# Second attention: a share of the squares one operation later on VectorE, and the weighted sums copied out by VectorE

## The chip, the cores and the metric

The program runs on one NeuronCore of one Trainium2 chip. The metric is the device time of one execution in microseconds (us); of three timed executions of the kernel before the median is 3164.51 us (3160.64 to 3164.62). Engines: PE is TensorE, DVE is VectorE, ACT is ScalarE, POOL is GpSimd, SP is SyncE, which only issues DMAs here.

## The reference

The model has six sublayers on 4 x 1024 tokens of width 128: a top-1 expert layer, causal attention, the top-1 expert layer again, a top-2 expert layer, a second attention with two kinds of weights, and the top-2 expert layer again. The change lies in the second attention alone (16 heads of width 8, no mask):

```python
S = jnp.einsum('bhnd,bhmd->bhnm', Q, K) / dh ** 0.5
W_tau = jax.nn.softmax(S, axis=-1)
W_sigma = 1.0 / ((1.0 + jnp.abs(S) / b_) ** 2 + t_ ** 2)
W_sigma = W_sigma / W_sigma.sum(axis=-1, keepdims=True)
tau   = jnp.einsum('bhnm,bhmd->bhnd', W_tau, V)
sigma = jnp.einsum('bhnm,bhmd->bhnd', W_sigma, V)
f = 0.5 * tau + 0.5 * sigma
```

## The kernel before, in words

`attend_both` runs the second attention. The batch and the heads give 64 heads to go through; each has 1024 queries and 1024 keys, in 8 tiles of 128. A *slot* is two tiles, so a head is four slots and the stage 256. Every engine runs its own loop over slots, written out by hand; semaphores alone tie them together, and each engine takes its instructions strictly in the order written. Within one body `j` different jobs belong to different slots (lags `LS` = 4, `LT` = `LE` = 6, `LP` = 7).

Per slot, each of the two halves `i`:

- PE computes three times a 128 x 1024 tile of scores: into `pm` for the row maxima, into `pb` for the softmax (with the negated maximum carried in extra rows of the stack), into `pa` for the absolute values. Then it *weighs*: `weigh` multiplies `Vh` (128 x 32) with the weights of an earlier slot and adds into `po` (L1786, 8 matmuls).
- DVE takes the row maximum of `pm` (L1927) and clears the sign of `pa` into the buffer `sg` (L1936). There are one `pm`, one `pa` and one `pb`, so PE waits with each until it has been read.
- ACT takes the exponential of `pb` into `pt` (L1849), and on the whole slot the logarithm and the exponential that make 1/(square + constant) out of the square (L1864, L1868).

The square is z(z + b), elementwise over a slot's 2 x 1024 columns. Its first 26/32 are POOL's, in two instructions: `shifted = z + b` (L1727) and `z * shifted` (L1730). The last 6/32 are DVE's, one `scalar_tensor_tensor` of 128 x 384 elements (L1942). Both engines read and write SBUF only here, and both wait for the second sign clearing of the slot.

Once a head, in these four slots (A is the slot with `j % 4 == 0`, then B, C, D):

- Slot D: PE finishes the head's last weighing in the first half (`pv_done`); the sums `po` (128 x 512) are copied to `osb` by ACT (L1856); the first weighing of the next head, in the second half of D, may not write `po` before (`pe.wait_ge(o_sb, h)`); after it PE transposes `osb` (L1832) into `ptr`.
- Slot A: `output` on DVE, four small instructions that divide by the sums and write the head's result (L1903 to L1914). In its second half PE transposes the maxima (L1817), and at the end of the slot DVE runs `negated`, four small instructions on 8 x 128 (L1883 to L1890) whose rows SP's DMAs put into the stacks.

DVE's row of a slot is thus: maximum, [`output`], sign, maximum, sign, square, [`negated`].

Of the kernel before, what the change touches and what calls it, by code (L numbers as in the profile page):

```python
# [11 lines left out]
ALU = mybir.AluOpType  # L12
ACT = mybir.ActivationFunctionType
# [3 lines left out]
B, T, D = 4, 1024, 128  # L17
# [3 lines left out]
TT = T // P  # L21
# [11 lines left out]
RING = 4  # L33
# [1605 lines left out]
def attend_both(nc, tag, V, F, par, qd, kd, ident, stacks, cleared):  # L1639
# [6 lines left out]
    PER = TT // 2  # L1646
    UNROLL = PER * RING
    LS, LT, LE, LP = 4, 6, 6, 7
    SC = DH ** -0.5
    CUT = 26 * T // 32  # L1650
    with ExitStack() as ctx:
# [3 lines left out]
        parh = m.sb("parh", [P, RING, 2])  # L1655
# [3 lines left out]
        sg = [m.sb(f"sg{r}", [P, 2, T]) for r in range(4)]  # L1659
        shifted = m.sb("shifted", [P, 2, CUT])  # L1660
        osb = m.sb("osb", [P, CH])
# [5 lines left out]
        po = m.ps("po", [P, CH])  # L1667
# [12 lines left out]
        def at(it, j, lag):  # L1680
            s = UNROLL * it + (j - lag)
            return None if isinstance(s, int) and not 0 <= s < SLOTS else s

        def head(it, j, lag):

            return RING * it + (j - lag) // PER
# [10 lines left out]
        def some(x, least=1):  # L1697

            return not (isinstance(x, int) and x < least)

        with nc.Block() as block:
# [136 lines left out]
            @block.scalar  # L1838
            def _(act):
                nc.scalar.preload_act_table_set("natural_log_exp_and_others")  # L1840

                def body(it, j):
                    st, se, so = at(it, j, LT), at(it, j, LE), at(it, j, LP + 1)
                    for i in range(2):
                        if st is not None:
                            act.wait_ge(tau_mm, 2 * st + i + 1)
                            if some(st, 4):
                                act.wait_ge(pv_done, 2 * (st - 4) + i + 1)
                            nc.scalar.activation(pt[(j - LT) % 4][:, i, :], pb[:], ACT.Exp, scale=SC)\  # L1849
                                .then_inc(tau_exp, 1)  # L1850
                        if i == 0 and so is not None and (j - LP - 1) % PER == PER - 1:
                            h = head(it, j, LP + 1)
                            act.wait_ge(pv_done, TT * h + TT)
                            if some(h):
                                act.wait_ge(o_turned, h)
                            nc.scalar.activation(osb[:], po[:], ACT.Copy).then_inc(o_sb, 1)  # L1856
                        if se is not None:
                            buf = sg[(j - LE) % 4]
                            if i == 0:
                                h = head(it, j, LE)  # L1860
                                act.wait_ge(sq_pool, se + 1)
                                act.wait_ge(sq_dve, se + 1)
                                act.wait_ge(par_ready, h + 1)
                                nc.scalar.activation(buf[:], buf[:], ACT.Ln,  # L1864
                                                     bias=parh[:, ((j - LE) // PER) % RING, 1:2]).then_inc(ln_done, 1)
                            else:
                                act.wait_ge(ln_done, se + 1)
                                nc.scalar.activation(buf[:], buf[:], ACT.Exp, scale=-1.0).then_inc(sig_done, 1)  # L1868

                slots(act, body)  # L1870

            @block.vector
            def _(dve):
                def negated(it, j):

                    if j % PER or at(it, j, 1) is None:
                        return
                    h, r = head(it, j, 1), ((j - 1) // PER - 1) % RING
                    top, rem = ptr[0:TT, 0:P], ptr[0:TT, P:2 * P]
                    dve.wait_ge(rows_turned, h + 1)  # L1880
                    if some(h):
                        dve.wait_ge(rows_in[r], 16 * SPLIT * (it + ((j - 1) // PER - 1) // RING + 1))
                    nc.vector.tensor_scalar(rows[:, 0, :], top, -1.0, None, ALU.mult).then_inc(chain, 1)  # L1883
                    dve.wait_ge(chain, 3 * h + 1)
                    nc.vector.scalar_tensor_tensor(rem, top, -1.0, rows[:, 0, :], ALU.mult, ALU.subtract)\
                        .then_inc(chain, 1)
                    dve.wait_ge(chain, 3 * h + 2)
                    nc.vector.tensor_copy(rows[:, 1, :], rem).then_inc(chain, 1)
                    dve.wait_ge(chain, 3 * h + 3)
                    nc.vector.tensor_tensor(rows[:, 2, :], rem, rows[:, 1, :], ALU.subtract).then_inc(rows_sb, 1)  # L1890

                def output(it, j, n):

                    if (j - LP - 2) % PER != PER - 1 or at(it, j, LP + 2) is None:
                        return
                    h = head(it, j, LP + 2)
                    o = ptr[:].rearrange("p (c q k) -> p c q k", c=4, q=4)
                    scale = rz[:].unsqueeze(3).broadcast_to([P, 4, 4, DH])
                    if n == 0:
                        dve.wait_ge(o_turned, h + 1)  # L1900
                        if some(h):
                            dve.wait_ge(weighed, 2 * h)
                        nc.vector.reciprocal(rz[:], o[:, :, :, DH]).then_inc(rz_done, 1)  # L1903
                    if n == 1:
                        dve.wait_ge(rz_done, h + 1)
                        if some(h):
                            dve.wait_ge(f_done, h)
                        nc.vector.tensor_tensor(fw[:], o[:, :, 0:2, 0:DH], scale[:, :, 0:2], ALU.mult)\
                            .then_inc(weighed, 1)
                        nc.vector.tensor_tensor(o[:, :, 2:4, 0:DH], o[:, :, 2:4, 0:DH], scale[:, :, 2:4], ALU.mult)\  # L1910
                            .then_inc(weighed, 1)
                    if n == 2:
                        dve.wait_ge(weighed, 2 * h + 2)
                        nc.vector.tensor_tensor(F[:, :, h, :].rearrange("p (s c) d -> p s c d", s=2),  # L1914
                                                o[:, :, 2:4, 0:DH].rearrange("p c s d -> p s c d"),
                                                fw[:].rearrange("p c s d -> p s c d"), ALU.add)\
                            .then_inc(f_done, 1)

                def body(it, j):
                    sm, ss = at(it, j, 0), at(it, j, LS)  # L1920
                    for i in range(2):
                        if sm is not None:
                            t = 2 * (j % PER) + i
                            dve.wait_ge(max_mm, 2 * sm + i + 1)
                            if i == 0 and j % PER == 0 and some(sm, 2 * PER):
                                dve.wait_ge(rows_turned, head(it, j, 0) - 1)
                            nc.vector.tensor_reduce(mx[:, (j // PER) % 2, t:t + 1], pm[:], AX.X, ALU.max)\  # L1927
                                .then_inc(max_red, 1)
                        if i == 0:
                            for n in range(3):  # L1930
                                output(it, j, n)
                        if ss is not None:
                            dve.wait_ge(abs_mm, 2 * ss + i + 1)
                            if some(ss, 4):
                                dve.wait_ge(pv_done, 2 * (ss - 4) + i + 1)
                            nc.vector.tensor_scalar(sg[(j - LS) % 4][:, i, :].bitcast(I32), pa[:].bitcast(I32),  # L1936
                                                    SIGN_OFF, None, ALU.bitwise_and).then_inc(abs_done, 1)
                    if ss is not None:
                        h, buf = head(it, j, LS), sg[(j - LS) % 4]
                        dve.wait_ge(abs_done, 2 * ss + 2)  # L1940
                        dve.wait_ge(par_ready, h + 1)
                        nc.vector.scalar_tensor_tensor(buf[:, :, CUT:T], buf[:, :, CUT:T],  # L1942
                                                       parh[:, ((j - LS) // PER) % RING, 0:1], buf[:, :, CUT:T],
                                                       ALU.add, ALU.mult).then_inc(sq_dve, 1)
                    negated(it, j)

                slots(dve, body)
        m.clear_sems()

# [167 lines left out]
```

## Time and profile before

| | |
|---|---|
| time, median of 3 | 3164.51 us |
| the profiled execution: its time, its span | 3132.56 us, 3130.8 us |
| busy share of the span | PE 80%, DVE 82%, ACT 72%, POOL 64% |
| second attention, first to last square on DVE | 1273.92 to 2803.41 us |
| DVE squares (L1942) | 256, mean 914 ns, from 617 to 2669 ns |
| POOL (L1727, L1730) | 256 each, mean 1838 and 3733 ns |

How to read it: busy shares are averages over stages with different limits. In the 40 slices of the span, the second attention fills slices 17 to 35, where DVE shows 9 tenths everywhere, and so do ACT and POOL. Below, a timeline row gives the start (us from the span's start), the duration (us), engine, line, operation, output<-input and count; a value in square brackets is how long the engine sat idle before it and what ended that.

### The profile page before, as it was taken

The numbers are of one execution on the slowest core, as the hardware profiler recorded it, in microseconds if no ns is written. First come the engines' busy times: TensorE is split into PE (matmuls) and PEld (weight loads), VectorE is DVE, ScalarE is ACT, GpSimd is POOL, SyncE is SP. The second block draws the span as 40 slices with busy tenths as digits, with TensorE's granted clock in tenths as the row PEclk, the third lists the DMA queues.
The fourth block names the chain that finished last, engine by engine and source line by source line (L and its number), as shares of the span: only waits on it lengthen the run. The fifth ranks groups of instructions, "written<-read, shape, count | busy, mean of one in ns | idle before, by whom it ended". The sixth has DMA issues, their size and how long they took to land. (4 is left out here: it accounts for less than half of the span.)

```text
span 3130.8 us, 61223 instructions
## 1 busy us (share of the span) xinstructions
PE 2497.2 (80%) x18663; PEld 1032.7 (33%) x18790; DVE 2578.9 (82%) x4251; ACT 2257.5 (72%) x2453; POOL 1995.7 (64%) x1350
## 2 busy tenths in 40 slices
PE   3655999997658984788888888888888888874899
PEld 3632333334654552122222222222222222213455
DVE  4666888885566656899999999999999999977665
ACT  4432777776444543599999999999999999992454
POOL 4510222222634441699999999999999999983444
PEclk9976999998778996799999999999999999995899
DMA  3222100010210002000000000000000000000000
GB/s 114 68 74 71 30 28 29 28 29 8 64 51 1 1 0 88 14 15 12 12 13 14 12 12 14 13 12 12 14 13 12 12 15 12 12 1 1 4 11 14
DMA packets 77234, 74.71 MB, mean 24 GB/s; under 512 B 16112, under 2 KB 57592, under 8 KB 76992
## 3 DMA queue, kind: packets, MB, share of 16 engines
q1 hardware_dynamic: 72832, 64.47, 7.0%
q0 software_dynamic: 4288, 8.82, 0.9%
q8 instruction: 59, 0.97, 0.1%
q14 instruction: 55, 0.45, 0.0%
HBM read 48.04 MB, written 24.42 MB: 23 GB/s over the span
## 5 line engine op out<-in xcount | busy, mean ns | idle before, releaser
L1730 POOL TENSOR_TENSOR a_sg<-a_sg,a_shifted 128x1664 f32<-128x1664 f32 x256 | 955.6, 3733 | 21.4
L1927 DVE TENSOR_REDUCE a_mx<-a_pm 128x1 f32<-128x1024 f32 x512 | 619.4, 1210 | 21.9 <-PE a_pm L1769 21.8
L1936 DVE TENSOR_SCALAR a_sg<-a_pa 128x1024 int32<-128x1024 int32 x512 | 619.2, 1209 | 4.2 <-PE a_pa L1769 3.9
L1849 ACT ACTIVATE a_pt<-a_pb 128x1024 f32<-128x1024 f32 x512 | 523.6, 1023 | 108.4 <-PE a_pb L1769 108.4
L1786 PE MATMUL a_po<-a_pt,a_Vh 128*32 128x512 f32 x2048 | 540.6, 607 | 2.2 <-ACT a_sg L1868 2.2
L1786 PE MATMUL a_po<-a_sg,a_Vh 128*32 128x512 f32 x2048 | 540.6, 607 | 0.0
L1727 POOL TENSOR_SCALAR a_shifted<-a_sg,a_parh 128x1664 f32<-128x1664 f32 x256 | 470.4, 1838 | 101.9 <-DVE a_sg L1936 64.2
L1864 ACT ACTIVATE a_sg<-a_sg,a_parh 128x2048 f32<-128x2048 f32 x256 | 511.9, 2000 | 0.0
L1868 ACT ACTIVATE a_sg<-a_sg 128x2048 f32<-128x2048 f32 x256 | 489.9, 1914 | 0.0
L1769 PE MATMUL a_pm<-all_K,all_Q 96*128 96x512 bf16 x1024 | 316.2, 391 | 149.9 <-DVE a_mx L1927 123.8
L1548 ACT ACTIVATE a_pt<-a_ring 128x1024 f32<-128x1024 f32 (+2 forms) x384 | 313.5, 846 | 167.4 <-PE a_ring L1475 164.1
L1625 DVE TENSOR_REDUCE a_mx<-a_ring 128x2 f32<-128x1024 f32 (+3 forms) x384 | 359.2, 955 | 77.2 <-PE a_ring L1458 52.8
L1769 PE MATMUL a_pa<-all_Q,all_K 96*128 96x512 bf16 x1024 | 311.4, 386 | 83.1 <-DVE a_sg L1936 65.9
L1383 POOL TENSOR_SCALAR_AFFINE_SELECT a_pt<-a_pt 128x256 f32<-128x256 f32 x256 | 104.0, 406 | 372.3 <-ACT a_pt L1548 372.0
L1769 PE MATMUL a_pb<-all_Q,all_K 128*128 128x512 bf16 x897 | 279.8, 381 | 13.7 <-ACT a_pt L1849 6.0
L1942 DVE SCALAR_TENSOR_TENSOR a_sg<-a_sg,a_parh 128x384 f32<-128x384 f32 x256 | 233.9, 914 | 15.7 <-POOL a_parh L1716 2.7
L1769 PEld LDWEIGHTS a_pm<-all_K,all_Q 96*128 96x128 bf16 x1024 | 63.6, 98 | 546.0 <-DVE a_mx L1927 522.7
L881 ACT ACTIVATE f_sg<-f_psg 128x512 f32<-128x512 f32 x176 | 105.1, 597 | 167.9 <-PE f_psg L840 166.9
L1492 PE MATMUL a_po<-a_pt,a_Vh 128*32 128x384 f32 (+3 forms) x1920 | 191.4, 437 | 1.9 <-POOL a_pt L1383 1.8
L804 POOL TENSOR_TENSOR f_hidl<-f_hid,f_hidh 128x512 f16<-128x512 f32 x88 | 101.9, 1157 | 124.5 <-ACT f_hidh L888 124.5
L1769 PEld LDWEIGHTS a_pa<-all_Q,all_K 96*128 96x128 bf16 x1024 | 79.5, 97 | 272.9 <-DVE a_sg L1936 232.3
L804 POOL TENSOR_TENSOR all_V<-f_hid,all_XNT 128x512 f16<-128x512 f32 x88 | 101.8, 1157 | 97.1 <-ACT all_XNT L888 97.1
(278 smaller groups left out, 4718.6 us busy)
## 6 DMA issues: line engine op xcount, KB each, us to landing
all_Q<-q_parts SPq DMA_DIRECT2D x256, 48.0 KB
all_K<-k_parts SPq DMA_DIRECT2D x256, 48.0 KB
k_parts<-p_parts SPq DMA_DIRECT2D x16, 384.0 KB, 2.8
all_Q<-a_rows SPq DMA_DIRECT2D x384, 2.0 KB
e_recs<-routed_rows SPq DMA_DIRECT2D x70, 64.5 KB, 1.8
n_xn<-expert_rows SPq DMA_DIRECT2D x16, 256.0 KB, 4.9
q_parts<-p_parts SPq DMA_DIRECT2D x16, 192.0 KB, 2.3
q_parts<-p_parts SPq DMA_DIRECT2D x8, 384.0 KB, 2.6
```

Of the source, the lines that this page charges most:

```text
L1548: nc.scalar.activation(pt[n % 4][:, :, ga:gb, c * P:CH], of_weight(y)[:, :, 0:(gb - ga) * width].rearrange("p u (g n) -> p u g n", n=width ...
L1625: nc.vector.tensor_reduce(mx[:, j % 2, half, :, strip_at(t)], of_maximum(y)[:, :, 0:min(CH, (t + 1) * P - half * CH)], AX.X, ALU.max).then ...
L1727: nc.gpsimd.tensor_scalar(shifted[:], buf[:, :, 0:CUT], b2, 1.0, ALU.add, ALU.mult)\
L1730: nc.gpsimd.tensor_tensor(buf[:, :, 0:CUT], buf[:, :, 0:CUT], shifted[:], ALU.mult)\
L1769: last = nc.tensor.matmul(out[:, lo:lo + CH], lhsT[0:rows_, t * P:(t + 1) * P], rhs[0:rows_, lo:lo + CH], start=True, stop=True)
L1786: last = nc.tensor.matmul(po[32 * q:32 * q + 32, :], Vh[:, ((j - lag) // PER) % 2, t, :], wts[:, i, half * CH:(half + 1) * CH], start=(t = ...
L1849: nc.scalar.activation(pt[(j - LT) % 4][:, i, :], pb[:], ACT.Exp, scale=SC)\
L1864: nc.scalar.activation(buf[:], buf[:], ACT.Ln, bias=parh[:, ((j - LE) // PER) % RING, 1:2]).then_inc(ln_done, 1)
L1868: nc.scalar.activation(buf[:], buf[:], ACT.Exp, scale=-1.0).then_inc(sig_done, 1)
L1927: nc.vector.tensor_reduce(mx[:, (j // PER) % 2, t:t + 1], pm[:], AX.X, ALU.max)\
L1936: nc.vector.tensor_scalar(sg[(j - LS) % 4][:, i, :].bitcast(I32), pa[:].bitcast(I32), SIGN_OFF, None, ALU.bitwise_and).then_inc(abs_done, 1)
L1942: nc.vector.scalar_tensor_tensor(buf[:, :, CUT:T], buf[:, :, CUT:T], parh[:, ((j - LS) // PER) % RING, 0:1], buf[:, :, CUT:T], ALU.add, AL ...
```

## The change

It does two things on DVE's and ACT's rows of the second attention; PE's and POOL's rows stay as they are. DVE's square of a slot no longer stands at the end of its slot but in the next slot's body, behind that slot's first maximum (the function `square`, called in the first half). The copy of `po` to `osb` leaves ACT's slot D and stands on DVE in slot D, behind the second maximum (`copy_out`).

```diff
@@ scalar
-                    st, se, so = at(it, j, LT), at(it, j, LE), at(it, j, LP + 1)
+                    st, se = at(it, j, LT), at(it, j, LE)
...
-                        if i == 0 and so is not None and (j - LP - 1) % PER == PER - 1:
-                            h = head(it, j, LP + 1)
-                            act.wait_ge(pv_done, TT * h + TT)
-                            if some(h):
-                                act.wait_ge(o_turned, h)
-                            nc.scalar.activation(osb[:], po[:], ACT.Copy).then_inc(o_sb, 1)
@@ vector
+                def copy_out(it, j):
+
+                    if (j - LP - 1) % PER != PER - 1 or at(it, j, LP + 1) is None:
+                        return
+                    h = head(it, j, LP + 1)
+                    dve.wait_ge(pv_done, TT * h + TT)
+                    if some(h):
+                        dve.wait_ge(o_turned, h)
+                    nc.vector.tensor_copy(osb[:], po[:]).then_inc(o_sb, 1)
+
+                def square(it, j):
+
+                    s = at(it, j, LS + 1)
+                    if s is None:
+                        return
+                    h, buf = head(it, j, LS + 1), sg[(j - LS - 1) % 4]
+                    dve.wait_ge(abs_done, 2 * s + 2)
+                    dve.wait_ge(par_ready, h + 1)
+                    nc.vector.scalar_tensor_tensor(buf[:, :, CUT:T], buf[:, :, CUT:T],
+                                                   parh[:, ((j - LS - 1) // PER) % RING, 0:1], buf[:, :, CUT:T],
+                                                   ALU.add, ALU.mult).then_inc(sq_dve, 1)
...
                         if i == 0:
+                            square(it, j)
                             for n in range(3):
                                 output(it, j, n)
+                        else:
+                            copy_out(it, j)
...
-                    if ss is not None:
-                        h, buf = head(it, j, LS), sg[(j - LS) % 4]
-                        dve.wait_ge(abs_done, 2 * ss + 2)
-                        dve.wait_ge(par_ready, h + 1)
-                        nc.vector.scalar_tensor_tensor(buf[:, :, CUT:T], buf[:, :, CUT:T],
-                                                       parh[:, ((j - LS) // PER) % RING, 0:1], buf[:, :, CUT:T],
-                                                       ALU.add, ALU.mult).then_inc(sq_dve, 1)
                     negated(it, j)
```

The first place is DVE's row from the start of slot D to the first sign clearing of slot A. `a_mx` are the row maxima, `a_sg` the buffer of absolute values and squares, `a_osb` the copied sums. Before:

```order
L1927 TENSOR_REDUCE a_mx<-a_pm 128x1
L1936 TENSOR_SCALAR a_sg<-a_pa 128x1024
L1927 TENSOR_REDUCE a_mx<-a_pm 128x1
L1936 TENSOR_SCALAR a_sg<-a_pa 128x1024
L1942 SCALAR_TENSOR_TENSOR a_sg<-a_sg,a_parh 128x2x192
L1927 TENSOR_REDUCE a_mx<-a_pm 128x1
L1903 RECIPROCAL a_rz<-a_ptr 128x16
```

Two signs, one square, and then the maximum of the next slot. The same place after:

```order
L1943 TENSOR_REDUCE a_mx<-a_pm 128x1
L1931 SCALAR_TENSOR_TENSOR a_sg<-a_sg,a_parh 128x2x192
L1955 TENSOR_SCALAR a_sg<-a_pa 128x1024
L1943 TENSOR_REDUCE a_mx<-a_pm 128x1
L1921 COPY a_osb<-a_po 128x512
L1955 TENSOR_SCALAR a_sg<-a_pa 128x1024
L1943 TENSOR_REDUCE a_mx<-a_pm 128x1
L1931 SCALAR_TENSOR_TENSOR a_sg<-a_sg,a_parh 128x2x192
L1897 RECIPROCAL a_rz<-a_ptr 128x16
```

The square of slot D now stands in slot A, one maximum later, and the copy stands between D's second maximum and its second sign.

The second place is DVE's row from the last sign of slot A over `negated` (the four instructions on `a_rows` and `a_ptr`) into slot B. Before:

```order
L1936 TENSOR_SCALAR a_sg<-a_pa 128x1024
L1942 SCALAR_TENSOR_TENSOR a_sg<-a_sg,a_parh 128x2x192
L1883 TENSOR_SCALAR a_rows<-a_ptr 8x128
L1885 SCALAR_TENSOR_TENSOR a_ptr<-a_ptr,a_rows 8x128
L1888 CAST a_rows<-a_ptr 8x128
L1890 TENSOR_TENSOR a_rows<-a_ptr,a_rows 8x128
L1927 TENSOR_REDUCE a_mx<-a_pm 128x1
L1936 TENSOR_SCALAR a_sg<-a_pa 128x1024
```

The square came directly behind the sign that it waits for. After:

```order
L1955 TENSOR_SCALAR a_sg<-a_pa 128x1024
L1877 TENSOR_SCALAR a_rows<-a_ptr 8x128
L1879 SCALAR_TENSOR_TENSOR a_ptr<-a_ptr,a_rows 8x128
L1882 CAST a_rows<-a_ptr 8x128
L1884 TENSOR_TENSOR a_rows<-a_ptr,a_rows 8x128
L1943 TENSOR_REDUCE a_mx<-a_pm 128x1
L1931 SCALAR_TENSOR_TENSOR a_sg<-a_sg,a_parh 128x2x192
L1955 TENSOR_SCALAR a_sg<-a_pa 128x1024
```

Here the square has moved past five instructions, the four of `negated` and B's first maximum. In slots B to D it moves past one.

## Rows read from the trace of the kernel before

**Rows 1.** Windows: busy us of each engine, TensorE's granted clock, DMA share, GB/s
```profile
1700.00:2000.00 300.00, 256.95 (x1434) 68.78 (x1461) 293.64 (x354) 285.08 (x212) 282.32 (x127) 1.00 0.04 12
```

**Rows 2.** Timeline, ACT: the copy in slot D of two heads in a row
```profile
2200.85 0.60 ACT L1856 ACTIVATE a_osb<-a_po 128x512 f32<-128x512 f32 x1
...
2224.90 0.60 ACT L1856 ACTIVATE a_osb<-a_po 128x512 f32<-128x512 f32 x1
```

**Rows 3.** Timeline, DVE: from slot D's square to slot B
```profile
2204.77 1.20 DVE L1942 SCALAR_TENSOR_TENSOR a_sg<-a_sg,a_parh 128x384 f32<-128x384 f32 x1
2205.89 1.21 DVE L1927 TENSOR_REDUCE a_mx<-a_pm 128x1 f32<-128x1024 f32 x1
2207.02 0.24 DVE L1903 RECIPROCAL a_rz<-a_ptr 128x16 f32<-128x16 f32 x1
2208.05 1.23 DVE L1936 TENSOR_SCALAR a_sg<-a_pa 128x1024 int32<-128x1024 int32 x1
...
2210.33 1.21 DVE L1936 TENSOR_SCALAR a_sg<-a_pa 128x1024 int32<-128x1024 int32 x1
2211.57 0.62 DVE L1942 SCALAR_TENSOR_TENSOR a_sg<-a_sg,a_parh 128x384 f32<-128x384 f32 x1
2212.11 0.27 DVE L1883 TENSOR_SCALAR a_rows<-a_ptr 8x128 bf16<-8x128 f32 x1
2213.26 1.20 DVE L1927 TENSOR_REDUCE a_mx<-a_pm 128x1 f32<-128x1024 f32 x1
```

**Rows 4.** Timeline, POOL: the same stretch
```profile
2201.81 3.74 POOL L1730 TENSOR_TENSOR a_sg<-a_sg,a_shifted 128x1664 f32<-128x1664 f32 x1
2205.80 1.68 POOL L1727 TENSOR_SCALAR a_shifted<-a_sg,a_parh 128x1664 f32<-128x1664 f32 x1 [0.25 <-POOL a_sg L1730]
2207.57 3.73 POOL L1730 TENSOR_TENSOR a_sg<-a_sg,a_shifted 128x1664 f32<-128x1664 f32 x1
2211.75 1.96 POOL L1727 TENSOR_SCALAR a_shifted<-a_sg,a_parh 128x1664 f32<-128x1664 f32 x1
```

**Rows 5.** Lines: count, busy us, mean ns, idle before
```profile
L1942 DVE SCALAR_TENSOR_TENSOR a_sg<-a_sg,a_parh 128x384 f32<-128x384 f32 x256 | 233.9, 914 | 15.7 <-POOL a_parh L1716 2.7
L1093 DVE COPY all_V<-p_psv 128x128 f32<-128x128 f32 x32 | 7.0, 279 | 0.0
```

**Rows 6.** Timeline, the stage's end: POOL's product and DVE's square that began inside it
```profile
2796.16 3.74 POOL L1730 TENSOR_TENSOR a_sg<-a_sg,a_shifted 128x1664 f32<-128x1664 f32 x1
2797.65 2.67 DVE L1942 SCALAR_TENSOR_TENSOR a_sg<-a_sg,a_parh 128x384 f32<-128x384 f32 x1
```

**Rows 7.** Timeline, PE: weighing, transposes and scores in slot D; then slot C
```profile
2204.07 0.66 PE L1832 MATMUL a_ptr<-all_ident,a_osb 128*128 128x128 f32 x4
2204.56 0.60 PE L1769 MATMUL a_pm<-all_K,all_Q 96*128 96x512 bf16 x2
...
2219.56 1.21 DVE L1936 TENSOR_SCALAR a_sg<-a_pa 128x1024 int32<-128x1024 int32 x1
2220.83 0.60 PE L1769 MATMUL a_pa<-all_Q,all_K 96*128 96x512 bf16 x2
2221.36 0.62 PE L1786 MATMUL a_po<-a_pt,a_Vh 128*32 128x512 f32 x2
2222.36 0.60 PE L1769 MATMUL a_pm<-all_K,all_Q 96*128 96x512 bf16 x2
```

**Rows 8.** Timeline, PE, and the window behind its wait, early in the stage
```profile
1301.16 0.62 PE L1769 MATMUL a_pm<-all_K,all_Q 96*128 96x512 bf16 x2 [1.79 <-DVE a_mx L1927]
...
1302.43 1.06 PE L1769 MATMUL a_pa<-all_Q,all_K 96*128 96x512 bf16 x2
1303.42 1.07 PE L1786 MATMUL a_po<-a_pt,a_Vh 128*32 128x512 f32 x2
...
1305.19 0.60 PE L1769 MATMUL a_pm<-all_K,all_Q 96*128 96x512 bf16 x2
...
1301.30:1304.70 3.40, 3.40 (x14) 0.68 (x12) 3.24 (x3) 2.21 (x3) 2.85 (x1) 0.55 0.04 5
```

## The prediction

> **What bounds the kernel now.** I read the 40 slices first: in the second attention three engines stand at nine tenths, so the busy shares don't name the bound. The window inside the stage [rows 1] puts DVE at 293.6 of 300 us, ACT at 285, POOL at 282. The timeline then decides. DVE starts each instruction 0.08 us before the last one's end (a 1.21 us maximum is followed after 1.13) and nowhere in a head do I find it idle [rows 3]. A head takes 2224.90 - 2200.85 = 24.05 us [rows 2]. DVE's row adds up to it: sixteen maxima and signs at 1.13 (18.08), `output` 1.03 (2207.02 to 2208.05), `negated` 1.15 (2212.11 to 2213.26), 4 x 0.12 because a square waits for its own sign to finish (1.24 instead of 1.13 behind it), and four squares, two of 0.54 and two of 1.12: 24.06.
>
> The two kinds of squares are what matters. All 256 have the same shape, their mean is 914 ns [rows 5]. In slot A it takes 0.62 us, in slot D 1.20. The long one begins at 2204.77, inside POOL's product, which ends at 2201.81 + 3.74 = 2205.55; the square ends at 2205.97, 0.42 behind it [rows 3, 4]. At the stage's end a square begins 1.49 us into a product, takes 2.67, and ends at 2800.32, again 0.42 behind the product's end at 2799.90 [rows 6]. So a square that begins while POOL multiplies does its work only when POOL's instruction is over. The other way round, POOL's `shifted`, 1.68 alone, takes 1.96 when it starts 0.18 behind a square [rows 3, 4]. Squares are short now because they are asked for in POOL's pauses or near a product's end. The question is where in POOL's row they fall after the change.
>
> The Trainium skill, page "SBUF — State Buffer", section "SBUF: two separate sides", says that DVE with two SBUF inputs and GpSimd contend for one port pair, an exclusive lock that the first to start holds "for the whole instruction; the other fully blocks". The two rows above agree as far as they reach, 2.25 us of waiting. Where the rule goes further: it gives the full 3.7 us for a square that starts just behind a product's start; going by the longest wait shown alone, each block below would end 1.3 us sooner, and two of them would cost 2.6 us a head less.
>
> **The change, part by part.** Let E be the end of a slot's second sign. POOL, if idle, starts `shifted` at E + 0.21 (2211.54 to 2211.75) and the product 1.77 later, at E + 1.98; the product ends at E + 5.71 [rows 3, 4].
>
> (a) Own wait removed: 4 x 0.12 = 0.48 us a head, a gain.
>
> (b) The copy, now on DVE. No row shows it. 128 elements out of PSUM take 0.28, a maximum over 1024 takes 1.21 [rows 3, 5]; these are the bounds, and the line through them gives 0.68 for 512 (ACT needs 0.60 [rows 2]). It holds DVE 0.60. On ACT it saves about as much, worth nothing, since ACT has idle time in the head.
>
> (c) PE behind the copy. The next head's first weighing waits for it. With `a` the start of D's first sign, DVE goes: maximum a + 1.13, copy a + 2.26 to 2.94, second sign a + 2.86, free a + 3.99. PE weighs from a + 3.00 for 1.00 us, transposes, starts the next `pm` 0.49 later, and DVE has it 0.60 after that [rows 7]: a + 5.09. DVE waits 1.10 us in front of A's first maximum. Before, the copy was done a slot half earlier and the square filled the gap.
>
> (d) The other slots. From the end of a first sign, PE needs 0.06 to `pa`, 0.53 to weighing, 1.00 to `pm`, 0.60 to the end: 2.19 [rows 7]; DVE, with no square left in between, is there after 2.18. Waits of 0.0 to 0.1, I take 0.06 in B and C.
>
> (e) The squares. In slot B the square of A begins at E - 0.08 + 1.15 (`negated`) + 1.13 (maximum) = E + 2.20. In slot A the square of D begins at E - 0.08 + 1.10 + 1.13 = E + 2.15. The product has begun at E + 1.98 in both. So both fall just behind the product's start, the worst place. DVE goes on at E + 5.71 + 0.42 - 0.08 = E + 6.05 and not at E + 2.69 or 2.74: 3.36 and 3.31 lost. Behind the square stand `output`, the sign, and with it `pa`, PE and the next slot. Such a block also keeps POOL idle, so that it is punctual for the next slot and the pattern repeats itself. In C and D the square begins at E - 0.08 + 0.06 + 1.13 = E + 1.11, inside `shifted`, which ends at E + 1.89; it goes then, and DVE continues at E + 2.23 instead of E + 1.65: 0.58 each, and 0.3 in D because POOL's product was put off by B's and C's squares.
>
> Sum with nothing else: DVE's row is 18.08 + 4 x 0.54 + 1.03 + 1.15 + 0.60 = 23.02, + 1.10 + 0.12 = 24.24, + 3.36 + 3.31 + 1.16 + 0.3 = 32.4 us a head.
>
> (f) PE's clock. In (e) PE waits from some 2.3 us into slots A and B until the late sign, 4 us and more. Early in the stage PE waited 1.79 us for DVE, and the granted clock then read 0.55 for 3.4 us (half, 1.2 GHz), with `pa` to weighing 0.99 and weighing to `pm` 1.77 [rows 8]. At that rate the path of (d) is 0.06 + 0.99 + 1.77 + 0.60 = 3.42 or more, DVE waits 1.2 before C's maximum, and C's square begins at E + 2.3, behind the product's start: C is blocked too, and D likewise. With all four blocked a slot runs from E to E in 6.05 + 1.13 + 1.13 + 1.21 = 9.52, a head in 4 x 9.52 + 1.03 + 0.60 = 39.7. Whether the half clock covers that path depends on when it sets in: after a wait of 4 us it may be partly over. I take it that C and D are blocked every other time: (32.4 + 39.7) / 2 = 36.05.
>
> (36.05 - 24.05) x 64 heads = +768 us. On the profiled execution, 3132.56, that is 3901. The median of the runs shown is 31.95 us above that execution; I put it on top: 3933.
>
> **Rivals.**
> 1. PE's clock comes back in time: two blocks a head, 32.4 us, +534, 3699. For it: PE has stood at full clock through the whole middle of the stage [rows 1].
> 2. All four slots blocked, 39.7 us, +1002, 4167. It would also come about if POOL's product gets in ahead of a square that waits out `shifted`. For it: the half clock after a wait of only 1.79 us. Against it: a pending square went 0.42 behind POOL's end both times.
> 3. Squares win the race. POOL's product starts only 0.17 and 0.22 us before them in (e). If POOL claims its operands later in its instruction than DVE, nothing is blocked in A and B: 24.24 + 1.16 + 0.3 = 25.7, +106, 3270. If only one of the two is blocked, about 29, +317, 3482.
> 4. Faster. If the next head's first weighing reaches PE over 1.1 us behind D's second maximum anyway, the copy hides in full, and if squares then meet no product either, DVE has 23.02 + 0.12 = 23.14 a head: -58 us, 3106. It decides in D: the gains are 0.48 from (a) and 2 x 0.58 from squares that are short again, the costs 0.60 for the copy and 0.12 in B and C, so DVE's wait of (c) must stay under 0.92. Against it: PE in D and C goes straight from `pa` to weighing [rows 7], and POOL, 1.77 + 3.73 + 0.25 a slot [rows 4], allows nothing under 23.0.
>
> **How the numbers follow.** Mixed blocks, the forecast: 0.46. Two only: 0.15. Four: 0.19. Squares win one or both races: 0.05 and 0.10. Faster: 0.04; the rest, 0.01, about equal. Most probable 3933. The range, 3640 to 4190, takes in the first three with their roundings (0.80). What 0.2% (6 us) can tell from no change: faster 0.04, same 0.01, slower 0.95, since every case but rival 4 has (c) in it.
>
> **What would show it.** Squares (now L1931) with a mean near 3 us instead of 0.9, in A and B near 4 us and each ending 0.42 behind a product's end; in C and D either 1.1 to 1.5 or again near 4. The copy at 0.68. PE idle before `pa` in A and B by 4 us, granted clock in the stage well under 1.00 (1.00 throughout would be rival 1). POOL's product unchanged at 3.7, idle before `shifted` grown by some 10 us a head. The forecast is wrong if squares stay under 1.3 us on average (rival 3), and the sum of (e) is wrong if a square that begins inside a product ends before it.

## The result, and the profile after

The kernel after takes 3790.45 us (median of 4, 3778.31 to 3802.10) against 3162.57 us (4 runs): ratio 1.1998, 95% interval 1.1978 to 1.2019, or 628 us slower (the two medians alone give 1.1985). The profiled execution took 3781.38 us, its span is 3779.7 us. The range was 3640 to 4190, the forecast 3933.

The page, parts 1 and 2: busy us of each engine; then, over 40 slices, DVE's busy tenths and TensorE's granted clock.

```profile
PE 2701.8 (71%) x18790; PEld 1069.0 (28%) x18790; DVE 3039.5 (80%) x4315; ACT 2239.2 (59%) x2389; POOL 1988.3 (53%) x1350
...
DVE  4658888646666799999898999999998999987765
...
PEclk9968999968798688888888888898888888888599
```

The window that answers to [rows 1]:

```profile
1700.00:2000.00 300.00, 208.57 (x1024) 52.85 (x1023) 272.67 (x256) 197.12 (x140) 197.50 (x89) 0.88 0.03 9
```

The same engines do less in the same 300 us, PE 209 instead of 257, and the clock is 0.88 instead of 1.00. Only DVE is still near full, and part 5 of the page says with what (busy us, mean ns | idle before, and what ended it):

```profile
L1730 POOL TENSOR_TENSOR a_sg<-a_sg,a_shifted 128x1664 f32<-128x1664 f32 x256 | 972.7, 3799 | 21.3
L1727 POOL TENSOR_SCALAR a_shifted<-a_sg,a_parh 128x1664 f32<-128x1664 f32 x256 | 423.5, 1654 | 731.9 <-DVE a_sg L1955 722.4
L1943 DVE TENSOR_REDUCE a_mx<-a_pm 128x1 f32<-128x1024 f32 x512 | 623.2, 1217 | 195.3 <-PE a_pm L1769 194.9
L1769 PE MATMUL a_pa<-all_Q,all_K 96*128 96x512 bf16 x1024 | 352.1, 429 | 554.8 <-DVE a_sg L1955 554.5
L1931 DVE SCALAR_TENSOR_TENSOR a_sg<-a_sg,a_parh 128x384 f32<-128x384 f32 x256 | 650.9, 2543 | 0.5 <-POOL a_parh L1716 0.3
```

The two waits for DVE's sign clearing (L1936, now L1955), in the kernel before:

```profile
L1727 POOL TENSOR_SCALAR a_shifted<-a_sg,a_parh 128x1664 f32<-128x1664 f32 x256 | 470.4, 1838 | 101.9 <-DVE a_sg L1936 64.2
L1769 PE MATMUL a_pa<-all_Q,all_K 96*128 96x512 bf16 x1024 | 311.4, 386 | 83.1 <-DVE a_sg L1936 65.9
```

The squares, same shape and count, went from 914 to 2543 ns [rows 5]. The added time is counted as busy although DVE waits in it: a reader of busy shares would miss it. POOL's idle time before `shifted` grew from 102 to 732 us, or 9.8 us a head, PE's in front of `pa` from 83 to 555 us.

The timeline of one head (start, duration), POOL and DVE from slot A into B:

```profile
2246.45 1.65 POOL L1727 TENSOR_SCALAR a_shifted<-a_sg,a_parh 128x1664 f32<-128x1664 f32 x1 [4.26 <-DVE a_sg L1955]
...
2248.18 3.72 POOL L1730 TENSOR_TENSOR a_sg<-a_sg,a_shifted 128x1664 f32<-128x1664 f32 x1
2248.47 3.85 DVE L1931 SCALAR_TENSOR_TENSOR a_sg<-a_sg,a_parh 128x384 f32<-128x384 f32 x1
```

The square starts 0.29 us behind the product and ends at 2252.32, 0.42 behind the product's end at 2251.90: the 0.42 of [rows 6]. It is no single case: 156 of the 256 squares begin inside a product, and each of them ends 0.41 or 0.42 us behind that product's end.

I took all squares of 60 heads in the middle of the stage, by the slot in which they run: in A 60 of 60 last over 2 us (mean 3.50), in B 60 of 60 (3.39), in C 26 of 60 (2.16), in D 5 of 60 (1.33). I call a square over 2 us *blocked*. By heads: 34 have A and B alone blocked and take 31.8 us, 21 have C too (36.3), and 5 have all four (41.1). A head takes 34.2 us on average, and 34.2 - 24.05 over 64 heads is 650 us, the 649 us between the two spans.

Slot D and the start of A, DVE, in a head where PE ran at full clock:

```profile
2162.50 0.68 DVE L1921 COPY a_osb<-a_po 128x512 f32<-128x512 f32 x1
2163.09 1.21 DVE L1955 TENSOR_SCALAR a_sg<-a_pa 128x1024 int32<-128x1024 int32 x1
2165.45 1.23 DVE L1943 TENSOR_REDUCE a_mx<-a_pm 128x1 f32<-128x1024 f32 x1 [1.14 <-PE a_pm L1769]
```

The copy takes 0.68 (0.68 was worked out), holds DVE 0.59, and DVE waits 1.14 behind it (1.10). Over the 60 heads, PE's clock not always full, that wait is 1.43 on average.

### The profile page after: what moved, and what is told of

Same layout as the page of the kernel before. It is cut to its first block and busy times, and to the rows that moved or that the text cites. A ratio compares the mean times of both kernels' runs of the same rounds, so it can differ in the third digit from the quotient of the medians.

```text
span 3779.7 us, 61410 instructions
## 1 busy us (share of the span) xinstructions
PE 2701.8 (71%) x18790; PEld 1069.0 (28%) x18790; DVE 3039.5 (80%) x4315; ACT 2239.2 (59%) x2389; POOL 1988.3 (53%) x1350
## 5 line engine op out<-in xcount | busy, mean ns | idle before, releaser
L1730 POOL TENSOR_TENSOR a_sg<-a_sg,a_shifted 128x1664 f32<-128x1664 f32 x256 | 972.7, 3799 | 21.3
L1727 POOL TENSOR_SCALAR a_shifted<-a_sg,a_parh 128x1664 f32<-128x1664 f32 x256 | 423.5, 1654 | 731.9 <-DVE a_sg L1955 722.4
L1769 PE MATMUL a_pa<-all_Q,all_K 96*128 96x512 bf16 x1024 | 352.1, 429 | 554.8 <-DVE a_sg L1955 554.5
L1786 PE MATMUL a_po<-a_pt,a_Vh 128*32 128x512 f32 x2048 | 628.6, 696 | 76.0 <-DVE a_osb L1921 73.6
L1931 DVE SCALAR_TENSOR_TENSOR a_sg<-a_sg,a_parh 128x384 f32<-128x384 f32 x256 | 650.9, 2543 | 0.5 <-POOL a_parh L1716 0.3
L1786 PE MATMUL a_po<-a_sg,a_Vh 128*32 128x512 f32 x2048 | 629.1, 697 | 0.0
L1955 DVE TENSOR_SCALAR a_sg<-a_pa 128x1024 int32<-128x1024 int32 x512 | 620.7, 1212 | 4.3 <-PE a_pa L1769 2.3
L1769 PE MATMUL a_pm<-all_K,all_Q 96*128 96x512 bf16 x1024 | 359.6, 438 | 29.2 <-DMA all_K<-k_parts 15.4
L1769 PE MATMUL a_pb<-all_Q,all_K 128*128 128x512 bf16 x1024 | 342.4, 419 | 7.2 <-ACT a_pt L1849 7.2
L1769 PEld LDWEIGHTS a_pa<-all_Q,all_K 96*128 96x128 bf16 x1024 | 89.0, 106 | 762.1 <-DVE a_sg L1955 682.6
L1786 PEld LDWEIGHTS a_po<-a_pt,a_Vh 128*32 128x32 f32 x2048 | 80.6, 114 | 324.7 <-issue 307.8
```

The costliest lines, as they stand in the source:

```text
L1727: nc.gpsimd.tensor_scalar(shifted[:], buf[:, :, 0:CUT], b2, 1.0, ALU.add, ALU.mult)\
L1730: nc.gpsimd.tensor_tensor(buf[:, :, 0:CUT], buf[:, :, 0:CUT], shifted[:], ALU.mult)\
L1769: last = nc.tensor.matmul(out[:, lo:lo + CH], lhsT[0:rows_, t * P:(t + 1) * P], rhs[0:rows_, lo:lo + CH], start=True, stop=True)
L1786: last = nc.tensor.matmul(po[32 * q:32 * q + 32, :], Vh[:, ((j - lag) // PER) % 2, t, :], wts[:, i, half * CH:(half + 1) * CH], start=(t = ...
```

## The experiments

All ratios are against the kernel before on the same chip; "head" is the mean over 60 heads in the middle of the stage in the profile (24.03 us before), and counts of blocked squares are of the same 60. Theory: a square that is asked for just behind the start of POOL's product waits for its end. Rivals: the copy is what costs; the new order as such costs; blocks come from a phase between the engines.

**The copy alone.** The squares go back to the end of their slot.

```diff
-                            square(it, j)
...
+                    if ss is not None:
+                        h, buf = head(it, j, LS), sg[(j - LS) % 4]
+                        dve.wait_ge(abs_done, 2 * ss + 2)
+                        dve.wait_ge(par_ready, h + 1)
+                        nc.vector.scalar_tensor_tensor(...).then_inc(sq_dve, 1)
```

> The copy on DVE as in the kernel after, every square back in its old place right behind the slot's second sign. Theory (squares that fall behind the start of POOL's product are what costs): no square waits for a whole product; squares 0.6 to 1.2 us. DVE's row is 18.08 + 0.48 + 2.16 + 1.03 + 1.15 + 0.60 = 23.5 us a head, DVE waits 0.4 us before slot A's maximum because the square fills part of PE's way behind the copy, and up to 1.1 us of lengthened squares in C and D stay: 23.9 to 25.1 us a head against 24.05, so 3155 to 3230 us. Rival (the copy and PE's wait behind it are the main loss, and long squares only follow from it): most of the loss stays, over 3500 us.

3228.24 us, 1.0223 (1.0205 to 1.0241); head 25.13 us, no square over 2 us. Its squares:

```profile
L1948 DVE SCALAR_TENSOR_TENSOR a_sg<-a_sg,a_parh 128x384 f32<-128x384 f32 x256 | 197.6, 772 | 14.0 <-POOL a_parh L1716 1.0
```

The copy with PE's wait behind it costs 2.2%, a ninth of the loss, at the upper end of what was expected. The wait in front of slot A's maximum, expected at 0.4 us, is 0.97 on average, 0.49 in one head and 2.01 in another, and the granted clock in the middle is 0.98, not 1.00: in some heads PE runs at the half clock for a while.

**The squares alone.** As in the kernel after, with the copy on ACT as before.

```diff
+                        if i == 0 and so is not None and (j - LP - 1) % PER == PER - 1:
...
+                            nc.scalar.activation(osb[:], po[:], ACT.Copy).then_inc(o_sb, 1)
...
-                        else:
-                            copy_out(it, j)
```

> The squares one operation later as in the kernel after, the copy back on ACT. Theory: without the copy DVE waits only some 0.5 us before slot A's maximum, so D's square is asked for at E + 1.55 (E: end of the slot's second sign), inside POOL's first instruction, and isn't blocked by the product; A's square, behind the four small instructions, still is, in every head. 28.0 us a head with no half clock behind the block, 29.4 with C blocked as often as in the kernel after: 3410 to 3510 us. Rival (the copy makes the blocks): no long squares, under 3250 us. Rival (the move alone makes them all): near 3790 us.

3630.56 us, 1.1490 (1.1467 to 1.1513), above what I expected. The place of the blocks is as expected in A (1 of 60 blocked, mean 0.85) and B (60 of 60, mean 3.84), and D (1 of 60). But in C 59 of 60 were blocked, more than in the kernel after. Head 31.65 us. The count in C was the wrong part of the expectation (28.0 or 29.4 us a head); the run with PE kept busy in B is for it.

**The square of slot A back in its place.** One square in four, in front of `negated`.

```diff
-                            square(it, j)
+                            if (j - LS - 1) % PER:
+                                square(it, j)
...
+                    if (j - LS) % PER == 0:
+                        square(it, j + 1)
                     negated(it, j)
```

> The kernel after, with one square in four, that of slot A, back behind its own second sign and in front of the four small instructions. Theory: A's square is short, slot B has no square, so PE has no long wait in B and C's square isn't blocked; D's square, behind the copy, still waits for the product in every head. 24.24 + 0.12 + 3.36 + 1.46 = 29.2 us a head: about 3490 us (3440 to 3540). Rival (blocks bring on each other, through POOL's and PE's state, and don't hang on the place of each square): still over 3650 us.

3468.84 us, 1.0978 (1.0956 to 1.1000), head 29.03 us (29.2). The moved-back square takes 0.63, C's and D's squares 1.09 and 1.39 and none is blocked, D's square, done in A, is blocked in 60 of 60 (3.12). One instruction in four slots, moved back past five, takes 322 us off: whether a square in A or B is blocked hangs on its own place. C's blocks are another matter: here, where B isn't blocked, C never is.

**One SBUF input.** The same place, length and buffer, but a reduction in place of the square.

```diff
-                    nc.vector.scalar_tensor_tensor(buf[:, :, CUT:T], buf[:, :, CUT:T],
-                                                   parh[:, ((j - LS - 1) // PER) % RING, 0:1], buf[:, :, CUT:T],
-                                                   ALU.add, ALU.mult).then_inc(sq_dve, 1)
+                    nc.vector.tensor_reduce(away[:], buf[:, :, CUT:T], AX.X, ALU.max).then_inc(sq_dve, 1)
```

> The kernel after, with each of DVE's squares replaced by a maximum over the same 128 x 384 elements of the same buffer in the same place: one SBUF input and a 128 x 2 output in place of two SBUF inputs and a 128 x 384 output. DVE's share of the squares is left out of the computation. Theory (a square waits because it has two SBUF inputs beside POOL): the replaced instruction takes 0.5 to 0.6 us wherever it falls, PE's granted clock is back at 1.00, and a head takes 24.24 us, with only the wait behind the copy left: 3160 to 3200 us. Rival (the new order itself, with the copy, holds PE and DVE up, whatever the square reads): over 3400 us.

3155.81 us, 0.9983 (0.9973 to 0.9994), head 24.01 us:

```profile
L1932 DVE TENSOR_REDUCE a_away<-a_sg 128x2 f32<-128x384 f32 x256 | 138.3, 540 | 0.9 <-POOL a_parh L1717 0.8
L1942 DVE TENSOR_REDUCE a_mx<-a_pm 128x1 f32<-128x1024 f32 x512 | 622.4, 1216 | 92.5 <-PE a_pm L1770 92.5
1700.00:2000.00 300.00, 255.67 (x1436) 69.57 (x1463) 281.22 (x365) 280.37 (x200) 273.37 (x127) 1.00 0.04 12
```

This decides between the theory and "the order as such": with the whole new order in place, copy included, the loss is gone as soon as the moved instruction reads one tensor from SBUF instead of two and writes next to nothing. It takes 0.53 to 0.55 wherever it falls, 68 times inside a product, and the clock is 1.00. The run can't tell the second input from the large output. DVE's sign clearings, whose one large input is in PSUM and whose 128 x 1024 output goes to SBUF, help: 137 of them lie wholly inside a product in the kernel after, and all take 1.20 to 1.23 us. So neither an SBUF input nor an SBUF output is blocked by itself; the two together, with no second input, were not run.

**PE kept busy in B, with the squares alone.** Twelve matmuls into `ptr`, which nobody reads there, in front of the `pa` for which PE waits.

```diff
+                        if i == 1 and j % PER == 1 and at(it, j, LP + 2) is not None and sm is not None:
+                            pe.wait_ge(rows_sb, head(it, j, 2) + 1)
+                            pe.wait_ge(f_done, head(it, j, LP + 3) + 1)
+                            for _ in range(12):
+                                nc.tensor.matmul(ptr[:], K[rm][0:96, 0:P], Q[rm][0:96, 0:CH], start=True, stop=True)
                         if ss is not None:
                             if some(2 * ss + i):
                                 pe.wait_ge(abs_done, 2 * ss + i)
```

> The kernel with the squares moved and the copy on ACT, plus twelve 512-column matmuls in slot B of each head, behind PE's second pb and in front of the pa for which PE waits 4 us; they go into ptr, which nobody reads then, and add nothing to the result. There, of the squares done in slot C, 60 of 61 had waited for a product. Theory (C is blocked only because PE's clock has fallen to half in B's wait, so that C's first maximum comes over 1 us late): granted clock near 1.00, the path from B's first late sign to C's maximum back from 3.3 to 4.0 us to some 2.25, C's square no longer blocked, a head 31.5 - 3.4 = 28.1 us, 3400 to 3450 us. Rival (C is blocked because a blocked slot B leaves POOL and DVE in a phase that blocks the next slot, whatever PE's clock): unchanged, 3630 us, or longer by the added matmuls.

3393.59 us, 1.0740 (1.0724 to 1.0757), 237 us less for 12 x 64 more matmuls. Windows of the middle, the squares alone and then with the added matmuls, and the matmuls themselves in one head:

```profile
1700.00:2000.00 300.00, 220.53 (x1097) 55.74 (x1115) 276.68 (x271) 223.13 (x164) 212.51 (x97) 0.90 0.03 9
```

```profile
1700.00:2000.00 300.00, 249.14 (x1390) 72.12 (x1389) 291.58 (x303) 248.45 (x184) 240.80 (x109) 1.00 0.04 11
```

```profile
2022.04 2.75 PE L1811 MATMUL a_ptr<-all_Q,all_K 96*128 96x512 bf16 x12
```

B is still blocked in 60 of 60 heads, C in none (59 before), and the time from the end of B's late sign to C's maximum is 2.23 to 2.24 us in all 60; without the added matmuls it was 3.31 to 3.97 in the heads with a blocked C. The head is 27.83 us (28.1). So C's blocks come from PE's clock, and B's don't: at 1.00 they are all still there.

**The same in the kernel after.**

> The kernel after, copy and squares as there, plus the same twelve matmuls in slot B of each head in front of the pa that PE waits for; the result is unchanged. Theory: PE's clock no longer falls behind B's block, so C's square, blocked in 26 of 60 heads, never is; A and B are still blocked in each head, by the order of DVE's row. That is the two-block head of the prediction, 32.4 us against 34.2 in the profile: about 3675 us. Rival (C's blocks come from the phase of POOL and DVE after B, not from the clock): 3790 us or more.

3659.52 us, 1.1590 (1.1572 to 1.1608). C is blocked in no head, D in none, B in 60, A in 57. Head 32.13 us: this is the two-block head of the prediction, summed up there to 32.4. C's blocks, and what comes with them, are thus worth 131 us of the 628. The clock in the middle is 0.92 still, and the wait in front of A's first maximum is 1.85 us on average: the matmuls stand in slot B alone, and nothing fills PE's wait in A.

**The product in two halves.**

```diff
-                    nc.gpsimd.tensor_tensor(buf[:, :, 0:CUT], buf[:, :, 0:CUT], shifted[:], ALU.mult)\
-                        .then_inc(sq_pool, 1)
+                    nc.gpsimd.tensor_tensor(buf[:, 0, 0:CUT], buf[:, 0, 0:CUT], shifted[:, 0], ALU.mult)
+                    nc.gpsimd.tensor_tensor(buf[:, 1, 0:CUT], buf[:, 1, 0:CUT], shifted[:, 1], ALU.mult)\
+                        .then_inc(sq_pool, 1)
```

> The kernel after, with POOL's product over 2 x 832 elements written as two instructions of 832 elements, with no wait between them. Theory (POOL holds what a square needs for the whole of one instruction, and lets it go between two): squares in A and B end 0.42 us behind the first half, so they take about 2.0 us instead of 3.4 to 3.9; PE's waits shrink with them. 24.24 + 2 x 1.6 + 1.5 = 28.9 us a head, 3430 to 3560 us. Rival (a waiting square gets in only when POOL has nothing queued): squares as long as before, 3790 us or more.

3508.11 us, 1.1106 (1.1086 to 1.1127), head 29.66 us. Squares' mean is 1587 ns; they take 1.77 in A and 2.03 in B. The head is 0.8 us over the 28.9 of the sum; the wait before A's first maximum alone is 2.10 us on average, where the sum has 1.10. POOL and DVE in a slot B:

```profile
2069.10 1.96 POOL L1730 TENSOR_TENSOR a_sg<-a_sg,a_shifted 128x832 f32<-128x832 f32 x1
2071.01 2.26 POOL L1731 TENSOR_TENSOR a_sg<-a_sg,a_shifted 128x832 f32<-128x832 f32 x1
```

```profile
2069.40 2.07 DVE L1932 SCALAR_TENSOR_TENSOR a_sg<-a_sg,a_parh 128x384 f32<-128x384 f32 x1
```

The first half ends at 2071.06, the square at 2071.47, 0.41 behind it, although POOL has the second half queued; that one takes 2.26 instead of about 2.0. What the square waits for is held for one instruction, and a square that waits goes in between two of them: of 121 squares that began inside a first half, 117 ended 0.41 to 0.48 us behind its end. The other 4 had begun in its last 0.1 us and waited out the second half as well; the last section has one.

**POOL's share, in the kernel before.** `CUT = 26 * T // 32` becomes 25, 24 and 23.

> The kernel before with 25/32 of a slot's columns squared by POOL instead of 26/32. Theory (in C and D squares are long only because POOL, at 5.75 us a slot, is behind DVE and still multiplies): POOL needs 5.56 us a slot, DVE's squares 0.69 instead of 0.62, the two long ones shrink from 1.2 towards 0.7: 23.2 to 23.6 us a head instead of 24.05, 3110 to 3135 us. Rival (DVE and POOL fall into the same phase at any share): 24.05 + 4 x 0.07 = 24.3, about 3180 us.

> The same with 24/32. Theory: POOL at 5.37 us a slot is never behind, no square waits, but each takes 0.75: DVE's row 22.90 + 4 x 0.13 = 23.4 us a head, 3120 us, about that of 25/32. Rival (same phase at any share): 24.6 us a head, about 3195 us.

> The kernel before with 23/32 of the columns squared by POOL. With 24/32 squares took 0.76 in A and B and 0.95 in C and D, 23.83 us a head. Theory (two things trade: every 1/32 less on POOL costs DVE 4 x 0.067 = 0.27 us a head, and shortens the two long squares until none waits): at 23/32 a square is 0.82 and none waits, 23.7 to 23.9 us a head, within 0.2% of 24/32, about 3145 us. Rival (the gain goes on as POOL gets lighter): 3135 us or less.

The last row was measured on another chip, where the kernel before took 3157.99 us.

| POOL's share | us | ratio, interval | head us | squares in A and B; C and D |
|---|---|---|---|---|
| 26/32 | 3159.3 | 1 | 24.03 | 0.62; 1.19 |
| 25/32 | 3150.66 | 0.9975 (0.9965 to 0.9985) | 23.94 | 0.69; 1.07 |
| 24/32 | 3143.98 | 0.9961 (0.9948 to 0.9975) | 23.83 | 0.76; 0.95 |
| 23/32 | 3147.11 | 0.9966 (0.9955 to 0.9976) | 23.82 | 0.83; 0.83 |

Here I was too hopeful: I took the waiting of C's and D's squares as pure loss and forecast 3110 to 3135 us for 25/32 and 3120 for 24/32, with no square waiting there; those of C and D still do (0.95). The long square shrinks by only 0.12 us for each 1/32 while the short ones grow by 0.07. 24/32 beats the kernel before by 0.4%, and its interval leaves 1 out; 23/32 is level with it, as expected.

## Why the prediction was right, and where it was off

- **What bounds the stage** and that the squares' length comes from POOL's product: right. The split product and the one-input run show it from two sides.
- **(b) and (c), the copy:** right in size, 0.68 and 1.14 measured for 0.68 and 1.10. With one SBUF input, where the clock is 1.00, the wait of (c) is 1.16 on average. In the kernel after it is 1.43, which the sum doesn't have. The copy alone gave 2.2%. (a) was not measured by itself.
- **(e), A and B:** right. Both blocked in 60 of 60 heads in the kernel after, though the margin was put at 0.17 and 0.22 us only. It was larger: the squares begin 0.7 us behind the product's start on average. Rival 3 fell. With C kept free the head is 32.13 us, for 32.4 summed. That this is so close is in part luck: in the 34 heads with A and B alone blocked (31.8 us) the two squares take 3.30 and 3.32 us where (e) has 3.98 and 3.93, and the waits before maxima take 2.19 us where (c) and (d) have 1.22.
- **(e), C and D unblocked:** squares of 1.09 and 1.39 us (the run with A's square moved back), where (e) comes to 0.62 + 0.58 = 1.20 and 1.50.
- **(f), the clock:** the mechanism is right, shown by the added matmuls. The size was off, and it was a guess: nothing in the rows gave "every other time". I had 36.05 us a head and squares of near 3 us on average; C was blocked in 26 of 60 heads, D in 5 of 60, a head took 34.2 us and a square 2.54. C was near the half, D far from it. Only where the path from the late sign (the first sign clearing behind a blocked square) to the next slot's first maximum took over 3 us was the square late enough (C: 3.43 to 3.80 when blocked, 2.23 to 2.66 when not; D: 3.02 to 3.16 when blocked, up to 3.04 when not).
- **Which heads have C blocked:** (f) has PE wait "4 us and more" in A and in B. In A it waits 3.99 us on average, in B only 2.66. The length of B's wait parts the heads without exception: the 26 with C blocked have 2.89 to 3.14 us, the 34 others 1.63 to 2.80. With the copy on ACT, where A isn't blocked, B's wait is 3.85 us or more in the 59 heads with C blocked, and 2.71 in the one without. The added matmuls cut B's wait to 1.3 us there, and no C is blocked. So the squares alone lose C nearly always because PE waits longer in B. Why it waits longer there is not shown by a run; it may be that PE comes out of an unblocked A at full clock and is done with its work in B sooner.
- **Where the 10.1 us a head of the profile went:** over the 60 heads, from the start of each DVE instruction to the next, squares hold DVE 10.07 us a head (3.30 before), waits before maxima 2.87 (none before), the copy 0.60, and 0.21 of idle time before squares is gone. That is 10.03 of the 10.13.
- **Rival 1** had two blocks a head, and the added matmuls produce that head, but at a clock of 0.92 and not 1.00; **rival 2** (all four blocked) held in 5 of 60 heads, at 41.1 us for its 39.7; **rival 4** failed on (c), as (c) itself measured 1.14 for its limit of 0.92, and on the squares, which did meet the product.

## What to carry to other kernels

Before moving a VectorE instruction with two SBUF inputs, lay it beside GpSimd's row and ask which GpSimd instruction will be running when it starts. A move past one to five instructions, out of a pause and behind the start of a 3.7 us one, cost 15% here, and it shows as busy time of an instruction whose shape has not changed; compare mean durations, not only idle time. If such an instruction can't be placed in a pause, cut the long GpSimd instruction in two (3790 to 3508 us here). A VectorE instruction with a single SBUF input is a third way; here that was shown for a reduction only, not for one that also writes a large SBUF tensor. And a wait that another engine's delay brings to PE can bring a second delay with it: look at the granted clock behind it.

## What the runs showed of the hardware that I had not expected

The order of the two starts decides, down to hundredths of a microsecond, and in both directions. DVE, then POOL, in slot C of a head with the clock at half:

```profile
2227.79 4.14 DVE L1931 SCALAR_TENSOR_TENSOR a_sg<-a_sg,a_parh 128x384 f32<-128x384 f32 x1
```

```profile
2227.80 3.72 POOL L1730 TENSOR_TENSOR a_sg<-a_sg,a_shifted 128x1664 f32<-128x1664 f32 x1
```

The square began 0.01 us first and waited out the whole product, to 0.41 behind its end. It is the only one: 18 other squares of this trace began 0.02 to 0.29 us ahead of a product, and all took 0.60 to 0.62 us. Their products then took 3.90 to 4.18 us, where one that meets no square takes 3.72: now POOL waited for DVE. So the start shown in the profile tells who wins, unless the two are within some hundredths of a microsecond. The Trainium skill, "SBUF — State Buffer", section "SBUF: two separate sides", gives the pair to "whichever ... starts first", and "for the whole instruction". The trace bears out both, the second at full length: 4.14 us for a 0.62 us instruction.

Between two GpSimd instructions without a wait between them the door is narrow. In the split product, this square began 0.01 us before the first half's end:

```profile
1767.13 2.34 DVE L1932 SCALAR_TENSOR_TENSOR a_sg<-a_sg,a_parh 128x384 f32<-128x384 f32 x1
```

It ended 0.41 behind the second half's end. So did the three others that began less than 0.1 us before the first half's end; every square that had begun 0.13 us or more before it got in.

And work added to PE made the program faster: 12 matmuls a head, 237 us less, because with them the granted clock in the middle was 1.00 and not 0.90, and C's squares were no longer blocked.
